# A decoder on one core: the scan layer L3_attn woven batch by batch into the steps of the slot layer L2_ffn

## The chip, the core and the metric

The kernel runs on 1 core of one Trainium2 chip. The time is the device time of one launch in microseconds. The kernel before took 3780.62 us (median of 3 runs, 3766.05 to 3781.16).

## What is computed

Four decoder levels of three layers each, one after another, on x of 8 batches x 256 tokens x 256 features in fp32. Every layer adds its result for layernorm(x) to x. The change concerns two neighbours: the slot layer L2_ffn, and the scan layer L3_attn behind it.

```python
# L2_ffn, X = layernorm(x); 1024 slots, hidden width 1024
xn, se = rms_norm(X, gamma_x), rms_norm(slot_embeds, gamma_slot)
logits = einsum('bsd,etd->bset', xn, se)
dispatch = softmax(logits, axis=1)                   # over the tokens
slots = einsum('bsd,bset->betd', xn, dispatch)
processed = gelu(slots @ w1) @ w2
combine = softmax(logits.reshape(b, s, e * t), axis=-1)   # over the slots
x = x + einsum('bnd,bsn->bsd', processed, combine)

# L3_attn, X = layernorm(x)
Z = layernorm(X) * gamma + beta
A = sigmoid(Z @ Wa.T + ba)
P = cumprod(A, axis=1)
S = cumsum((Z @ Wb.T + bb) / (P + 1e-8), axis=1)
x = x + (Z @ Wc.T + bc) * (P * (h0 + S)) + X
```

Both layers are independent from batch to batch. Within a batch, the scan needs the finished x of the slot layer.

## The kernel before

Everything stays in on-chip memory; one function for each layer and engine is written out in the engine's own queue, and every order between engines is a semaphore. `sig.up(name)` raises one, `sig.at(name, lane, trip, n)` is the value to wait for. There is no scheduler: the order in each queue is the order of the code. `Chain.link` (used for short dependent operations on VectorE) raises a semaphore and waits for it on the same engine. PSUM has 8 banks of 128 x 512 fp32 (`k.ps`).

**The slot layer** works in steps. A step finishes batch e (its inner products) and starts batch f = e + 1 (its logits and softmaxes). TensorE's pieces alternate between the two:
- `hidden_tensor`: slots @ w1, eight outputs for each half of the slots, in banks 4 and 5 by turns; ScalarE reads each with Gelu (`gelu_scalar`, L3320).
- `slot_zT_tensor` (L351): four transposes of f's normalized batch into bank 0.
- `logits_tensor`: banks 0 to 3; VectorE takes their maxima (L3400) and copies them (L3402), ScalarE takes the exponentials (L3338), VectorE scales them (L3404, L3405).
- `logits_turn_tensor` and `dispatch_turn_tensor` (L3226), 16 transposes each: logits, and dispatch weights; VectorE takes maxima (L3408), ScalarE the combine weights (L3344); both engines copy the turned dispatch weights (L3351, L3414).
- `processed_tensor`: hidden @ w2 in banks 6 and 7, four outputs a half, copied by VectorE (L3382).
- `slots_tensor`, `combine_turn_tensor` (L3264), and `combined_tensor`: the result in bank 6, which VectorE adds to x (L3421) ahead of its copy of combine weights (L3428).

A first step starts batch 0, a hardware loop (`Fori`) runs seven steps, a last one finishes batch 7. On VectorE a step opens with f's layernorm (L335) and RMS norm (L3156 to L3161, with the reciprocal root by ten short operations, L268 to L272).

**The scan layer** begins when all of x is there: statistics of the last tiles, the norms of all 16 tiles in one go (`norms_vector`), then a loop of four trips with two batches each, in banks 0 to 3 and 4 to 7. For each batch: a layernorm from those norms (L335), a second one (L279 to L288), four transposes (L351), two reads by ScalarE (L3494), 12 matmuls for a, b and c (L360), six reads by ScalarE (L3502), and on VectorE two running products (L3529), an addition, a reciprocal (L3532), a product, two running sums (L3535), L3538 and L3541; four transposes back (L3482), and two additions (L3546, L3547). The next layer, L3_xattn, starts with `norms_vector` again (L317, L324).

Nearly all matmuls go through one helper, so they have one line: `proj_feature` and `products` record L360. A matmul of fp32 operands is two records in the trace; a transpose is one.

## Time and profile before

| | |
|---|---|
| median of 3 runs | 3780.62 us |
| the profiled execution: device time, span | 3774.22 us, 3772.3 us |
| TensorE busy | 3108.0 us (82%) |
| VectorE busy | 1841.8 us (49%) |
| ScalarE busy | 1276.4 us (34%) |
| GpSimd busy | 439.8 us (12%) |
| mean granted TensorE clock | 0.897 |

Times inside the execution are microseconds from the start of its span. The slot layer's seven looped steps run from about 2537 to 3128, its last one to 3194, the scan layer from there to 3363. PE is TensorE (PEld its weight loads), DVE VectorE, ACT ScalarE, SP SyncE, which issues the DMAs. A busy share is an average over stages with different limits; the change is in one stretch, so its windows and its timeline say more. A granted clock of 1.00 is 2.4 GHz, 0.50 is 1.2 GHz, and what lies between is a mean over a stretch with both.

### The profile page before, as it was taken

The numbers are of one execution on the slowest core, as the hardware profiler recorded it, in microseconds if no ns is written. First come the engines' busy times: TensorE is split into PE (matmuls) and PEld (weight loads), VectorE is DVE, ScalarE is ACT, GpSimd is POOL, SyncE is SP. The second block draws the span as 40 slices with busy tenths as digits, with TensorE's granted clock in tenths as the row PEclk, the third lists the DMA queues.
The fourth block names the chain that finished last, engine by engine and source line by source line (L and its number), as shares of the span: only waits on it lengthen the run. The fifth ranks groups of instructions, "written<-read, shape, count | busy, mean of one in ns | idle before, by whom it ended". The sixth has DMA issues, their size and how long they took to land.

```text
span 3772.3 us, 54488 instructions
## 1 busy us (share of the span) xinstructions
PE 3108.0 (82%) x21063; PEld 2108.0 (56%) x21063; DVE 1841.8 (49%) x6353; ACT 1276.4 (34%) x2052; POOL 439.8 (12%) x454
## 2 busy tenths in 40 slices
PE   6999999589888788688862898959999998449877
PEld 3666668455554455455541565636666665336665
DVE  4443433699883466534449686542222221663323
ACT  1222213255554232133320686423233221224333
POOL 0001011123333000000001565000000000000000
PEclk9999999789898898799985899989999999669877
DMA  2000000100000000000000101000000000000000
GB/s 108 1 1 1 1 1 1 44 1 2 1 1 29 27 1 1 1 1 1 1 4 16 28 25 42 2 9 1 0 0 0 0 0 14 0 7 2 1 11 11
DMA packets 21697, 37.38 MB, mean 10 GB/s; under 512 B 2084, under 2 KB 19685, under 8 KB 20456
## 3 DMA queue, kind: packets, MB, share of 16 engines
q1 hardware_dynamic: 20664, 34.02, 2.7%
q8 instruction: 145, 2.38, 0.3%
q14 instruction: 72, 0.59, 0.1%
q10 hardware_dynamic: 816, 0.39, 0.0%
...
## 4 chain that ended last, share of the span: by engine, by line
PE 67%; DVE 22%; ACT 5%; issue 4%; DVEq 0%; SPq 0%; DMA 0%; POOL 0%; ACTq 0%; POOLq 0%
PE ps L360 38%; DVE arena L509 3%; DVE arena L1552 2%; PE ps L555 2%; ACT arena L590 2%; PE ps L457 2%; PE ps L2658 2%; PE ps L2001 2%; PE ps L2047 2%; PE ps L2677 2%; PE ps L602 2%; DVE arena L1543 2%; PE ps L643 2%; PE ps L1235 1%; PE ps L494 1%
## 5 line engine op out<-in xcount | busy, mean ns | idle before, releaser
L360 PE MATMUL ps<-weights,arena 128*128 128x256 f32 (+6 forms) x2592 | 722.2, 428 | 23.6 <-ACT arena L1369 7.6
L360 PE MATMUL ps<-arena,weights 128*128 128x256 f32 (+4 forms) x1936 | 611.9, 469 | 37.5 <-DMA fp_bias<-in_fp_bias 27.4
L360 PEld LDWEIGHTS ps<-weights,arena 128*128 128x128 f32 (+2 forms) x2592 | 484.7, 199 | 201.1 <-issue 110.3
L360 PEld LDWEIGHTS ps<-arena,weights 128*128 128x128 f32 (+1 forms) x1936 | 384.6, 209 | 225.1 <-issue 121.7
L360 PE MATMUL ps<-arena 128*128 128x256 f32 (+3 forms) x1592 | 416.0, 416 | 48.7 <-DVE arena L1822 43.4
L360 PEld LDWEIGHTS ps<-arena 128*128 128x128 f32 (+2 forms) x1592 | 297.3, 189 | 154.4 <-issue 68.1
L509 DVE TENSOR_REDUCE arena<-ps 128x16 f32<-128x1232 f32 (+2 forms) x96 | 179.1, 1866 | 204.4 <-PE ps L479 56.9
L590 ACT ACTIVATE arena<-ps 77x2048 f32<-77x2048 f32 (+1 forms) x112 | 209.9, 1874 | 171.6 <-PE ps L555 154.9
L1552 DVE MATCH_REPLACE8 arena<-arena 128x77 f32<-128x77 f32 x1024 | 215.2, 227 | 0.0
L771 POOL TENSOR_TENSOR x<-x,weights 128x512 f32<-128x512 f32 x32 | 40.7, 1272 | 1448.0 <-DVE arena L737 1448.0
L2014 ACT ACTIVATE arena<-ps 128x1536 f32<-128x1536 f32 x128 | 185.5, 1451 | 58.4 <-PE ps L2003 51.0
L643 PE MATMUL ps<-ident,arena 128*128 128x128 f32 x480 | 89.5, 316 | 106.3 <-DVE arena L737 41.8
L2032 POOL TENSOR_SCALAR_AFFINE_SELECT arena<-arena 128x512 f32<-128x512 f32 x128 | 152.5, 1192 | 116.6 <-ACT arena L2014 115.8
L1543 DVE MAX8 arena<-arena 128x8 f32<-128x77 f32 x1024 | 149.9, 227 | 11.4 <-ACT arena L1097 11.4
L351 PE MATMUL ps<-ident,arena 128*128 128x128 f32 x192 | 46.3, 398 | 118.2 <-DVE arena L288 45.9
L643 PEld LDWEIGHTS ps<-ident,arena 128*128 128x128 f32 x480 | 59.5, 158 | 147.7 <-issue 113.1
L3382 DVE COPY arena<-ps 128x1024 f32<-128x1024 f32 x16 | 19.6, 1225 | 244.7 <-PE ps L360 244.7
L555 PE MATMUL ps<-arena 32*77 32x256 f32 (+2 forms) x1792 | 131.7, 394 | 0.0
L2023 DVE TENSOR_TENSOR arena<-arena 128x512 f32<-128x512 f32 x128 | 88.4, 691 | 75.1 <-ACT arena L2014 74.3
L3320 ACT ACTIVATE arena<-ps 128x512 f32<-128x512 f32 x128 | 75.7, 597 | 130.3 <-PE ps L360 130.1
L457 PE MATMUL ps<-masks,identb 128*128 128x256 bf16 (+1 forms) x384 | 79.5, 333 | 48.6 <-DVE arena L509 26.6
L2001 PE MATMUL ps<-arena 12*128 12x256 bf16 x512 | 103.5, 279 | 10.0 <-DMA arena<-arena 9.8
...
## 6 DMA issues: line engine op xcount, KB each, us to landing
...
weights<-in_w_L_ffn SPq DMA_DIRECT2D x1, 3848.0 KB, 11.5
...
```

Of the source, the lines that this page charges most:

```text
L360: ins = k.nc.tensor.matmul(out, lhsT, rhs, start=start and i == 0, stop=i == n - 1)
L457: k.nc.tensor.matmul(out, k.identb[:, :], mask, start=True, stop=False, skip_group_check=True)
L509: k.nc.vector.tensor_reduce(out, src, AX, ALU.max).then_inc(*s.sig.up(u.a.p + "top"))
L555: ins = k.nc.tensor.matmul(k.ps[0:u.a.nk, HI + i, out], kT[group(i)], qT[group(i)], start=False, stop=True, skip_group_check=True)
L590: k.nc.scalar.activation(out, k.ps[0:u.a.nk, HI:HI + 4, :], ACT.Exp, scale=u.a.scale)\
L643: ins = k.nc.tensor.transpose(out[:, (2 * c + t) * P:(2 * c + t + 1) * P], src[:, t, c * P:(c + 1) * P], k.ident[:, :])
L1543: ins = v.max(tops_of_half(s, t, half, i)[:, h, :], of_half(s, t, half)[:, h, :])
L1552: ins = v.match_replace(left, tops_of_half(s, t, half, i)[:, h, :], left, -BIG)
L2001: mm(k.ps[:, base + u // 2, u % 2 * SEQ:(u % 2 + 1) * SEQ], kk[:, 0:P], q, start=True, stop=True, skip_group_check=True)
L2014: k.nc.scalar.activation(s.prob[at % PROBS], k.ps[:, base:base + 3, :].rearrange("p b f -> p (b f)"), ACT.Exp, scale=NH1 ** -0.5).then_inc ...
L2023: k.nc.vector.tensor_tensor(diag, diag, s.seen.unsqueeze(1).broadcast_to([P, 4, P]), ALU.min)\
L2032: k.nc.gpsimd.affine_select(diag, diag, [[0, 4], [1, P]], ALU.is_ge, 0.0, base=0, channel_multiplier=-1)\
```

## The change

The scan layer's own stage is gone, with its norms over all tiles. The slot layer is written out in ten steps instead of a loop: step `s` finishes batch e = s - 1, starts batch f = s, and carries the scan of batch n = s - 2, each where it exists. So steps 2 to 7 carry all three, step 8 carries e = 7 and n = 6, step 9 only n = 7. The scan of a batch calculates both layernorms itself. Its transposed z goes to bank 7, a and b to banks 4 and 5 (once the last gelu of the half has read them), c to bank 4 once a has been read, and the result's transposes to bank 4. `done` is now raised by the scan's last addition, the slot layer's own one raises `slotted`. The statistics of the finished batch for the next layer are taken at its end, so that L3_xattn takes none itself. SyncE loads the weights of L3_xattn after the last `slotted`; TensorE waits for the scan's weights before step 0.

```diff
-    prep = Signals(k.signals, "L2_ffn", 1, 1, se=1, seT_ps=1, seT=1, done=1, dve_step=k.steps["slots_prep"])
+    prep = Signals(k.signals, "L2_ffn", 1, 1, se=1, seT_ps=1, seT=1, dve_step=k.steps["slots_prep"])
     sig = Signals(k.signals, "L2_ffn", B, 1, z=1, zT_ps=1, zT=1, lT_ps=1, ex=1, l=1, l_ps=1, cmax=1, comb=1,
                   disp=1, dispT_ps=1, dispT_a=1, dispT_v=1, slots_ps=1, slots=1, combT_ps=1, combT_a=1, combT_v=1,
-                  hid_ps=16, hid=16, proc_ps=2, proc=2, out_ps=1, done=1, dve_step=k.steps["L2_ffn"])
-    return Bag(norms=norms, buf=buf, prep=prep, sig=sig)
+                  hid_ps=16, hid=16, proc_ps=2, proc=2, out_ps=1, slotted=1, dve_step=k.steps["L2_ffn"],
+                  g_z=1, g_zT_ps=1, g_zT=1, g_ab_ps=1, g_a=1, g_b=1, g_c_ps=1, g_c=1, g_o=1, g_out_ps=1,
+                  g_step=34, done=1, stats=1)
+    k.stats_ready["L3_attn"] = sig.at("stats", 0, B - 1, 1)
+    return Bag(norms=norms, buf=buf, g=g, prep=prep, sig=sig)
...
             pe.wait_ge(*s.sig.at("slots", 0, e, 1))
+            if e >= 2:
+                pe.wait_ge(*s.sig.at("done", 0, e - 2, 1))
+        if n == 8 and e:
+            pe.wait_ge(*s.sig.at("g_b", 0, e - 1, 1))
+            pe.wait_ge(*s.sig.at("g_c", 0, e - 1, 1))
...
-            pe.wait_ge(*s.sig.at("done", 0, e, 0))
+        elif e:
+            pe.wait_ge(*s.sig.at("slotted", 0, e - 1, 1))
...
+def scan_z_tensor(k, pe, s, n):
+    pe.wait_ge(*s.sig.at("g_z", 0, n, 1))
+    turn_tensor(k, s.g.zn, k.ps[:, 7, :]).then_inc(*s.sig.up("g_zT_ps"))
+def scan_in_tensor(k, w, src, b):
+    for c in range(KC):
+        ins = proj_feature(k, k.ps[:, b, c * SEQ:(c + 1) * SEQ], w_of(k, "L3_attn", w, KC), src, c * P, P)
+    return ins
+def scan_ab_tensor(k, pe, s, n):
+    pe.wait_ge(*s.sig.at("g_zT", 0, n, 1))
+    if n + 1 < B:
+        pe.wait_ge(*s.sig.at("hid", 0, n + 1, 8))
+    scan_in_tensor(k, "wa", s.g.zT, 4)
+    scan_in_tensor(k, "wb", s.g.zT, 5).then_inc(*s.sig.up("g_ab_ps"))
+def scan_c_tensor(k, pe, s, n):
+    pe.wait_ge(*s.sig.at("g_a", 0, n, 1))
+    scan_in_tensor(k, "wc", s.g.zT, 4).then_inc(*s.sig.up("g_c_ps"))
+def scan_out_tensor(k, pe, s, n):
+    pe.wait_ge(*s.sig.at("g_o", 0, n, 1))
+    if n + 1 < B:
+        pe.wait_ge(*s.sig.at("hid", 0, n + 1, 16))
+    for t in (0, 1):
+        for c in range(KC):
+            ins = k.nc.tensor.transpose(k.ps[:, 4, (2 * t + c) * P:(2 * t + c + 1) * P],
+                                        s.g.b[:, c, t * P:(t + 1) * P], k.ident[:, :])
+    ins.then_inc(*s.sig.up("g_out_ps"))
...
-    enter(k, pe, s.sig)
-    slots_step_tensor(k, pe, s, None, 0, first=True)
-    with pe.Fori(0, B - 1) as trip:
-        slots_step_tensor(k, pe, s, trip, trip + 1)
-    slots_step_tensor(k, pe, s, B - 1, None)
+    pe.wait_ge(*s.prep.at("seT", 0, 0, 1))
+    pe.wait_ge(*k.loaded["L3_attn"])
+    for step in range(B + 2):
+        e, f, n = in_steps(step - 1), in_steps(step), in_steps(step - 2)
+        if e is not None:
+            hidden_tensor(k, pe, s, e, 0, 0, 4)
+        if f is not None:
+            slot_zT_tensor(k, pe, s, f)
+        if e is not None:
+            hidden_tensor(k, pe, s, e, 0, 4, 8)
+        if n is not None:
+            scan_z_tensor(k, pe, s, n)
+        if f is not None:
+            logits_tensor(k, pe, s, f)
+        if n is not None:
+            scan_ab_tensor(k, pe, s, n)
+        if e is not None:
+            processed_tensor(k, pe, s, e, 0, 0, 2)
+        if n is not None:
+            scan_c_tensor(k, pe, s, n)
+        if e is not None:
+            processed_tensor(k, pe, s, e, 0, 2, 3)
+        if f is not None:
+            logits_turn_tensor(k, pe, s, f)
+        if e is not None:
+            processed_tensor(k, pe, s, e, 0, 3, 4)
+            hidden_tensor(k, pe, s, e, 1, 0, 4)
+        if f is not None:
+            dispatch_turn_tensor(k, pe, s, f)
+        if e is not None:
+            hidden_tensor(k, pe, s, e, 1, 4, 8)
+        if f is not None:
+            slots_tensor(k, pe, s, f)
+        if e is not None:
+            processed_tensor(k, pe, s, e, 1, 0, 4)
+        if n is not None:
+            scan_out_tensor(k, pe, s, n)
+        if f is not None:
+            combine_turn_tensor(k, pe, s, f)
+        if e is not None:
+            combined_tensor(k, pe, s, e)
...
+def scan_z_scalar(k, act, s, n):
+    act.wait_ge(*s.sig.at("g_zT_ps", 0, n, 1))
+    for c in range(KC):
+        ins = k.nc.scalar.activation(s.g.zT[:, c, :], k.ps[:, 7, c * SEQ:(c + 1) * SEQ], ACT.Identity,
+                                     bias=col_of(k, "L3_attn_be", c), scale=col_of(k, "L3_attn_g", c))
+    ins.then_inc(*s.sig.up("g_zT"))
+def scan_in_scalar(k, dst, b, fn, bias):
+    for c in range(KC):
+        ins = k.nc.scalar.activation(dst[:, c, :], k.ps[:, b, c * SEQ:(c + 1) * SEQ], fn, bias=col_of(k, bias, c))
+    return ins
+def scan_ab_scalar(k, act, s, n):
+    act.wait_ge(*s.sig.at("g_ab_ps", 0, n, 1))
+    if n:
+        act.wait_ge(*s.sig.at("g_out_ps", 0, n - 1, 1))
+    scan_in_scalar(k, s.g.a, 4, ACT.Sigmoid, "L3_attn_ba").then_inc(*s.sig.up("g_a"))
+    scan_in_scalar(k, s.g.b, 5, ACT.Identity, "L3_attn_bb").then_inc(*s.sig.up("g_b"))
+def scan_c_scalar(k, act, s, n):
+    act.wait_ge(*s.sig.at("g_c_ps", 0, n, 1))
+    scan_in_scalar(k, s.g.c, 4, ACT.Identity, "L3_attn_bc").then_inc(*s.sig.up("g_c"))
...
+            gelu_scalar(k, act, s, e, 0, 4, 8)
+        if n is not None:
+            scan_z_scalar(k, act, s, n)
+            scan_ab_scalar(k, act, s, n)
...
+            ins.then_inc(*sig.up("ex"))
+        if n is not None:
+            scan_c_scalar(k, act, s, n)
...
+def scan_z_vector(k, dve, s, n, ch):
+    v, g = k.nc.vector, s.g
+    tiles = [k.xs[:, SPARE + 2 * n + t, :] for t in (0, 1)]
+    dve.wait_ge(*s.sig.at("slotted", 0, n, 1))
+    if n:
+        dve.wait_ge(*s.sig.at("done", 0, n - 1, 1))
+        dve.wait_ge(*s.sig.at("g_zT_ps", 0, n - 1, 1))
+    for src, dst in ((tiles, g.z), ([g.z[:, 0, :], g.z[:, 1, :]], g.zn)):
+        hold(k, dve, "vector")
+        for t in (0, 1):
+            ins = v.bn_stats(g.st[:, t, :], src[t])
+        ch.link(ins)
+        hold(k, dve, "vector")
+        for t in (0, 1):
+            ins = v.bn_aggr(g.mv[:, t, :], g.st[:, t, :])
+        ch.link(ins)
+        ch.link(v.tensor_scalar(g.var, g.mv[:, :, 1], LN_EPS, None, ALU.add))
+        rsqrt(k, ch.link, g.rstd, g.var, g.t)
+        hold(k, dve, "vector")
+        for t in (0, 1):
+            ins = v.tensor_scalar(dst[:, t, :], src[t], g.mv[:, t, 0:1], g.rstd[:, t:t + 1], ALU.subtract, ALU.mult)
+        if dst is g.z:
+            ch.link(ins)
+    ins.then_inc(*s.sig.up("g_z"))
+def scan_sums_vector(k, dve, s, n, ch, part):
+    v, g = k.nc.vector, s.g
+    if part == 0:
+        dve.wait_ge(*s.sig.at("g_a", 0, n, 1))
+        for c in range(KC):
+            ins = v.tensor_tensor_scan(g.prod[:, c, :], g.a[:, c, :], g.ones, 1.0, ALU.mult, ALU.mult)
+        ch.link(ins)
+        ch.link(v.tensor_scalar(flat(g.a), flat(g.prod), 1e-8, None, ALU.add))
+        ch.link(v.reciprocal(flat(g.a), flat(g.a)))
+    else:
+        dve.wait_ge(*s.sig.at("g_b", 0, n, 1))
+        ch.link(v.tensor_tensor(flat(g.a), flat(g.b), flat(g.a), ALU.mult))
+        for c in range(KC):
+            ins = v.tensor_tensor_scan(g.sum[:, c, :], g.a[:, c, :], g.ones, 0.0, ALU.add, ALU.mult)
+        ch.link(ins)
+        for c in range(KC):
+            ins = v.scalar_tensor_tensor(g.b[:, c, :], g.sum[:, c, :], col_of(k, "L3_attn_h0", c), g.prod[:, c, :],
+                                         ALU.add, ALU.mult)
+        ch.link(ins)
+        dve.wait_ge(*s.sig.at("g_c", 0, n, 1))
+        v.tensor_tensor(flat(g.b), flat(g.b), flat(g.c), ALU.mult).then_inc(*s.sig.up("g_o"))
+def scan_done_vector(k, dve, s, n, ch):
+    v, g, x = k.nc.vector, s.g, x_at(k, n)
+    dve.wait_ge(*s.sig.at("g_out_ps", 0, n, 1))
+    ch.link(v.tensor_tensor(g.z, g.z, k.ps[:, 4, :].rearrange("p (t d) -> p t d", t=2), ALU.add))
+    v.tensor_tensor(x, x, g.z, ALU.add).then_inc(*s.sig.up("done"))
+    ch.close()
+    batch_stats_vector(k, dve, s, n)
...
+            rms_vector(k, ch, buf.z, buf.zn, buf.sq, buf.norm, 2).then_inc(*sig.up("z"))
+        if n is not None:
+            scan = Chain(dve, sig, 0, n, "g_step")
+            scan_z_vector(k, dve, s, n, scan)
...
+            processed_vector(k, dve, s, e, 0)
+        if n is not None:
+            scan_sums_vector(k, dve, s, n, scan, 0)
+        if f is not None:
+            dve.wait_ge(*sig.at("dispT_ps", 0, f, 1))
+            v.tensor_copy(buf.disp[:, 1, :], flat(k.ps[:, 2:4, :])).then_inc(*sig.up("dispT_v"))
+        if n is not None:
+            scan_sums_vector(k, dve, s, n, scan, 1)
+        if e is not None:
+            processed_vector(k, dve, s, e, 1)
+        if n is not None:
+            scan_done_vector(k, dve, s, n, scan)
```

Lines of the new kernel that the pieces below name: L3241 and L3279 are the old L3226 and L3264; L643 is the turn of the scan's z, L3316 the turn of its result; L3467 is the old L3382, L3572 the old L3414.

TensorE, the middle of a step. Before, in the loop, from the last matmuls of the first hidden half to the turn of the logits:

```order
L360 MATMUL ps<-arena,weights 128x512 x2
L360 MATMUL ps<-arena 128x256 x16
L3185 REGISTER_ALU
L3189 REGISTER_ALU
L360 MATMUL ps<-weights,arena 128x256 x24
L3232 REGISTER_ALU
L3226 MATMUL ps<-ident,arena 128x128 x16
L360 MATMUL ps<-weights,arena 128x256 x8
```

Now, in step 2, the same stretch:

```order
L360 MATMUL ps<-arena,weights 128x512 x8
L643 MATMUL ps<-ident,arena 128x128 x4
L360 MATMUL ps<-arena 128x256 x16
L360 MATMUL ps<-arena,weights 128x256 x8
L360 MATMUL ps<-weights,arena 128x256 x16
L360 MATMUL ps<-arena,weights 128x256 x4
L360 MATMUL ps<-weights,arena 128x256 x8
L3241 MATMUL ps<-ident,arena 128x128 x16
L360 MATMUL ps<-weights,arena 128x256 x8
```

The turn of the scan's z stands ahead of the logits, the eight matmuls of a and b behind them, and the four of c inside the inner products.

VectorE, between the maxima of the turned logits and the copies of inner products. Before:

```order
L3408 TENSOR_REDUCE arena<-ps 128x2
L3381 REGISTER_ALU
L3382 COPY arena<-ps 128x1024
L3413 REGISTER_ALU
L3414 COPY arena<-ps 128x1024
L3381 REGISTER_ALU
L3382 COPY arena<-ps 128x1024
```

Now, in step 2 (the first form of L3504 and L3512 are the running product and sum):

```order
L3564 TENSOR_REDUCE arena<-ps 128x2
L3467 COPY arena<-ps 128x1024
L3504 SCALAR_TENSOR_TENSOR arena<-arena 128x256 x2
L3506 TENSOR_SCALAR arena<-arena 128x512
L3507 RECIPROCAL arena<-arena 128x512
L3572 COPY arena<-ps 128x1024
L3510 TENSOR_TENSOR arena<-arena 128x512
L3512 SCALAR_TENSOR_TENSOR arena<-arena 128x256 x2
L3515 SCALAR_TENSOR_TENSOR arena<-arena,cols 128x256 x2
L3519 TENSOR_TENSOR arena<-arena 128x512
L3467 COPY arena<-ps 128x1024
```

The scan's sums stand in two parts, around the copy of the turned dispatch weights.

ScalarE, from the first half's gelus to the combine weights. Now, in step 2; before, L3338 with its table load stood directly behind the gelus, and L3344 behind L3338:

```order
L3378 ACTIVATE arena<-ps 128x512 x4
L3384 ACTIVATE arena<-ps,cols 128x256 x2
L3391 ACT_TABLE_LOAD
L3391 ACTIVATE arena<-ps,cols 128x256 x4
L3434 ACT_TABLE_LOAD
L3434 ACTIVATE arena<-arena 128x256 x8
L3391 ACTIVATE arena<-ps,cols 128x256 x2
L3443 ACTIVATE arena<-ps,arena 128x1024 x2
```

The reads of z, a and b stand ahead of the exponentials (now L3434), the read of c ahead of the combine weights (now L3443).

## Rows read from the trace of the kernel before

**Rows 1.** The profile's page: shares of the chain that ended last, by engine.

```profile
PE 67%; DVE 22%; ACT 5%; issue 4%; DVEq 0%; SPq 0%; DMA 0%; POOL 0%; ACTq 0%; POOLq 0%
```

**Rows 2.** Windows: stretch, length, busy time of each engine, clock, DMA share, GB/s.

```profile
2876.50:2960.70 84.20, 81.99 (x326) 56.90 (x325) 20.32 (x32) 24.66 (x46) 0.00 (x0) 1.00 0.00 0
3204.80:3245.50 40.70, 16.81 (x65) 13.48 (x66) 29.65 (x68) 9.20 (x18) 0.00 (x0) 0.67 0.00 0
3204.80:3210.50 5.70, 2.01 (x8) 1.61 (x9) 5.10 (x23) 1.02 (x2) 0.00 (x0) 0.50 0.00 0
3210.50:3217.70 7.20, 7.20 (x27) 6.07 (x26) 0.36 (x2) 2.31 (x3) 0.00 (x0) 0.74 0.00 0
2160.00:2220.00 60.00, 59.73 (x822) 37.44 (x822) 48.10 (x73) 48.39 (x40) 38.02 (x32) 1.00 0.09 24
```

**Rows 3.** Waits of one slot step, 2876.5 to 2960.7: total us, times, longest.

```profile
DVE arena L3400 <- PE ps L360: 14.0, 1, 14.0
...
DVE arena L3414 <- PE ps L3226: 8.0, 1, 8.0
DVE x L3421 <- PE ps L360: 7.7, 1, 7.7
...
PE ps L351 <- DVE arena L3161: 1.9, 1, 1.9
```

**Rows 4.** Timeline of that slot step: start, us, engine, line, work, [idle before].

```profile
2878.76 0.74 DVE L335 TENSOR_SCALAR arena<-x,norm,rstd 128x256 f32 x2 [1.02 <-issue]
...
2883.15 0.62 DVE L3161 TENSOR_SCALAR arena<-arena 128x256 f32<-128x256 f32 x2
...
2883.99 0.65 PE L351 MATMUL ps<-ident,arena 128*128 128x128 f32 x4 [1.87 <-DVE arena L3161]
...
2891.35 7.07 PE L360 MATMUL ps<-arena 128*128 128x256 f32 x32
...
2898.26 10.52 PE L360 MATMUL ps<-weights,arena 128*128 128x256 f32 x48
...
2902.98 0.51 ACT L3338 ACTIVATE arena<-arena 128x256 f32<-128x256 f32 x1 [9.53 <-DVE arena L3402]
...
2908.62 1.91 PE L3226 MATMUL ps<-ident,arena 128*128 128x128 f32 x16
...
2915.81 1.28 ACT L3320 ACT_TABLE_LOAD   x1 [0.62 <-PE ps L360]
...
2917.10 1.09 ACT L3320 ACTIVATE arena<-ps 128x512 f32<-128x512 f32 x2
...
2917.76 3.70 PE L360 MATMUL ps<-arena,weights 128*128 128x512 f32 x8 [0.34 <-ACT arena L3320]
```

**Rows 5.** Timeline of the last slot step's end and the scan stage.

```profile
3142.22 14.08 PE L360 MATMUL ps<-weights,arena 128*128 128x256 f32 x64 [0.69 <-ACT arena L3320]
...
3193.48 0.88 DVE L3421 SCALAR_TENSOR_TENSOR x<-ps,arena,x 128x256 f32<-128x256 f32 x2 [7.41 <-PE ps L360]
...
3200.68 0.75 DVE L279 BATCH_NORM_STATS2 arena<-arena 128x6 f32<-128x256 f32 x2
...
3204.04 0.73 DVE L288 TENSOR_SCALAR arena<-arena 128x256 f32<-128x256 f32 x2
...
3204.83 1.11 PE L351 MATMUL ps<-ident,arena 128*128 128x128 f32 x4 [11.50 <-DVE arena L288]
...
3205.98 1.02 ACT L3494 ACTIVATE arena<-ps,cols 128x256 f32<-128x256 f32 x2 [5.24 <-PE ps L351]
...
3220.04 1.28 DVE L3529 TENSOR_TENSOR_SCAN arena<-arena 128x256 f32<-128x256 f32 x2 [9.18 <-ACT arena L3502]
...
3228.90 1.12 PE L3482 MATMUL ps<-ident,arena 128*128 128x128 f32 x4 [6.03 <-DVE arena L3541]
...
3361.94 0.69 DVE L3547 TENSOR_TENSOR x<-x,arena 128x512 f32 x1
...
3365.19 1.17 DVE L324 BATCH_NORM_AGGREGATE norm<-stats 128x2 f32<-128x6 f32 x16 [0.15 <-DVE stats L317]
```

More of the change, by code:

```diff
@@ L3365, in L2_ffn_scalar @@
-def L2_ffn_scalar(k, act, s):
-    a = k.nc.scalar.activation
     enter(k, act, s.prep)
@@ L3436, in L2_ffn_vector @@
     enter(k, dve, s.prep)
     norms_vector(k, dve, s.norms)
[L3438 removed]
+    v.memset(buf.m, 0.0)
+    v.memset(s.g.ones, 1.0)
+    rms_vector(k, prep, buf.slots, buf.slots, buf.out, buf.norm, SC).then_inc(*s.prep.up("se"))
     dve.wait_ge(*s.prep.at("seT", 0, 0, 1))
[L3440 to L3443 removed]
@@ L3444, in L2_ffn_vector @@
-    with dve.Fori(0, B - 1) as trip:
-        slots_step_vector(k, dve, s, trip, trip + 1)
-    slots_step_vector(k, dve, s, B - 1, None)
-def scan_plan(k):
-    c, bufs = lane_buffers(k)
-    for buf in bufs:
-        buf.zn = c.take(2, D)
-        buf.a, buf.b, buf.c = c.take(KC, SEQ), c.take(KC, SEQ), c.take(KC, SEQ)
-        buf.prod, buf.sum = c.take(KC, SEQ), c.take(KC, SEQ)
-    ones = c.take(SEQ)
-    norms = norms_plan(k, "L3_attn")
-    prep = Signals(k.signals, "L3_attn", 1, 1, done=1)
-    sig = Signals(k.signals, "L3_attn", B // 2, 2, z=1, zT_ps=1, zT=1, abc_ps=1, abc=1, o=1, out_ps=1, done=1,
-                  dve_step=k.steps["L3_attn"])
-    return Bag(norms=norms, bufs=bufs, ones=ones, prep=prep, sig=sig)
```

302 lines of the change are left out of this document (90 added, 212 removed).

## Prediction

> **What bounds the kernel now.** I read the chain that ended last first: it runs through TensorE for 67% of the span and through VectorE for 22% [rows 1]. So a change counts where it shortens TensorE's own stream, or a place where TensorE waits for VectorE. Next the windows of the two stages that are woven together. In a slot step of 84.2 us TensorE is busy for 82.0 us at a granted clock of 1.00, VectorE for 20.3 and ScalarE for 24.7; in a trip of the scan stage, 40.7 us for two batches, TensorE is busy for 16.8 us at 0.67 and VectorE, with 29.7 us, leads [rows 2]. The first stage is a full TensorE beside an idle VectorE, the second a chain between engines. Then the waits of a slot step: VectorE waits 14.0, 8.0 and 7.7 us for TensorE at its reads of logits (L3400), turned dispatch weights (L3414) and output (L3421); TensorE waits once for VectorE, 1.9 us, for z [rows 3]. The timeline last, for where each new piece falls.
>
> **What goes.** From VectorE's add at the end of the last slot step (3193.48) to the norms of the next layer (L324 at 3365.19) it is 171.7 us [rows 5]. After the change the same stretch holds one batch's scan alone (step 9). The rest of the scan work has to fit into eight slot steps.
>
> **Step 9, one scan alone.** From the last slot add: 0.9 for the add and 0.15 for the hold behind it. Two layernorms: one runs from 3200.68 to the end of L288 at 3204.77, 4.1 us [rows 5], so 8.2; each new pass has a hold ahead of its statistics and one ahead of its apply, which I estimate at 0.12 each from the 0.15 that stands idle ahead of L324 [rows 5], so 8.7. Transposes 1.1 and ScalarE's copy 1.0 [rows 5]. The products for a and b are 16 matmul records. TensorE has been idle about 10 us by then, as it was for 11.5 us before the row at 3204.83, after which the granted clock was 0.50 for 5.7 us and 0.74 over the next 7.2, that is about 3.7 us at 1.2 GHz and the rest at 2.4 [rows 2, 5]. A record takes 0.216 us at full clock (48 between 2898.26 and 2908.62 [rows 4]), 0.43 at half: 3.7 us give 8.6 records, the other 7.4 take 1.6, together 5.3 (bounds 3.5 and 6.9). Sigmoid 0.9; the two reads of the same size at 3205.98 take 1.02. VectorE's sums from scan to product, 3220.04 to the transposes at 3228.90, 8.9 [rows 5]. Transposes 1.1, two adds 1.4 (L3547 takes 0.69), then the rest up to L324: today 2.6 from the end of the last add (3362.63) to 3365.19 with four statistics in it, of which two are left, so 1.7: 1.05 + 8.7 + 1.1 + 1.1 + 5.3 + 0.9 + 8.9 + 1.1 + 1.4 + 1.7 = 31.3 us; with links, 31.5 (29.5 to 34). The product with c hides behind the sums. Gain here: 171.7 - 31.5 = 140.2 us.
>
> **A full step (steps 2 to 7, six of them).** TensorE gets 24 records of 0.216, 5.2 us, and eight transposes of 0.11 (16 between 2908.62 and the next matmul take at most 1.9 [rows 4]), 0.9: 6.1 us. TensorE is busy for 97% of a step, so all of it lengthens the step; banks 4, 5 and 7 are free at those places. Waits:
> - z of the slot batch. VectorE idles 1.0 us at the top of a loop trip (L335 at 2878.76) and TensorE then 1.87 us for it at 2883.99 [rows 4]. Without a loop I leave about 0.2 of the 1.0: 0.8 us gained.
> - z of the scan batch is new. Its 8.7 us stand right behind the slot batch's z, which ended at 2883.77 and will at 2883.0; so it is there at 2891.7, and 0.2 later TensorE can start. TensorE arrives there 0.8 before 2891.35, at 2890.6: a wait of 1.3 us (bounds 0 and 2.6). Behind this wait stand the logits, which need nothing of it.
> - ScalarE. Products for a and b end 3.4 us behind the logits; sigmoid and identity take 1.8, the switch to Exp 1.3, so Exp starts at logits + 6.6, where it was + 4.7 (2902.98 against 2898.26 [rows 4]). Exponentials, maxima and combine weights move back by 2 us, but TensorE's turn of the logits moves back by 5.2 (a, b and c stand ahead of it), so that it still sets the maxima. Combine weights end at logits + 22.1, the first hidden product at + 22.4: today ScalarE reads it after a table load that waits for it (2915.81, [rows 4]); in the new order that load waits only for the inner products and starts at 22.1. TensorE's 0.34 us wait at 2917.76 and the pause of its weight loads there shrink: 0.3 gained.
> - VectorE's sums. The first half (scan, add, reciprocal: about 5.2 of the 8.9 us) stands behind the copy of the inner products, in the 8.0 us that VectorE waits ahead of L3414; the second half (3.7) behind that copy, where nothing is late; the two adds and the statistics (2.4) in the 7.7 us ahead of L3421 [rows 3]. Nothing on the path; without that cover each would cost its length.
> Sum: 6.1 - 0.8 + 1.3 - 0.3 = 6.3, and 0.2 less for the rests of the loop that TensorE's and ScalarE's queues had: 6.1 us a step (4.8 to 8), 36.6 for six.
>
> **Step 8** has no slot batch ahead of the scan's z, so that comes in time. TensorE waits instead for ScalarE's 0.8 us copy with its semaphores, 1.3 us, has 3.4 + 1.7 for its products and 0.4 for the transposes ahead of them; the transposes behind fall into the wait for VectorE's last copy. The new products cover the 0.69 us for the last gelu (3142.22, [rows 5]). 6.2 us (5 to 7.5).
>
> **Steps 0 and 1** carry no scan: -1.0 us (a z that comes earlier, and a memset and waits gone). The load of the scan's weights and SyncE's queue stand as they did.
>
> **The sum.** -140.2 + 36.6 + 6.2 - 1.0 = -98.4 us. On the profiled execution's own 3774.2 us that is 3675.8. The median of the three runs is 6.4 above the profiled execution, their lowest 8.2 below, so I put the median between, at 3679.
>
> **A page that speaks against it.** ScalarE changes tables three times in a step, before and after (the load at the loop's top goes, one ahead of the sigmoid comes), but two of the three then stand where ScalarE has little time to spare. In this trace the load at 2915.81 takes 1.28 us and the activation starts at 2917.10, 0.01 us behind its end [rows 4]. The Trainium skill (ScalarE: Activation LUTs, What ACT_TABLE_LOAD costs) gives the same 1283 ns, but adds about 1380 ns of drain to every switch. By that page, the switch to Exp and the next to Gelu would each be later by 1.4 us, TensorE would wait some 2.8 us more in a step, and the sum would end near 3696; the trace doesn't bear the drain out.
>
> **Rivals.**
> - ScalarE becomes late. Its queue has a and b ahead of Exp and c ahead of the combine weights. The margin is thin: combine weights at 22.1, first hidden product at 22.4. If ScalarE's new pieces take 2 us more (a load of 1.28 that is not hidden ahead of the sigmoid, and 0.7 of semaphores), TensorE waits 2 us a step at its third hidden product: 6 x 2 = 12, 3691. For it: the four waits between engines in a row. Against: 9.5 us idle ahead of Exp today [rows 4].
> - TensorE's clock. If the new pause made it fall, each step would lose what the spell at 0.50 to 0.74 cost: 3.7 us at half clock lose 1.9 us of work [rows 2]. Once or twice a step that is 11 to 22 us: 3690 to 3701. Against: with a pause of 1.87 us in each step the clock stands at 1.00.
> - No new wait. VectorE is ready before TensorE, and a step costs 4.8: 3671.
> - Slower than before: VectorE's queue in series. The scan's layernorms stand ahead of the logits' maxima and its sums ahead of the copies that TensorE's dispatch needs. The place from which it decides: 171.7 - 31.5 - 6.2 + 1.0 = 135 us over six steps, 22.5 us a step. All of VectorE's new work is 8.7 + 8.9 + 2.4 = 20.0; were all of it on the path beside TensorE's 6.1, a step would grow by 26.1 and the kernel end at 3799. Against: 29.7 us of idle at three places of the same step [rows 3].
> - The unrolled code is not there in time for an engine. At 5 us a step, 3714. Against: a stage with 822 matmul records in 60 us, written out too, keeps TensorE busy for 59.7 [rows 2].
>
> **How the numbers follow.** Forecast 0.64 (own range 3661 to 3695: six steps at 4.8 to 8, step 9 at 29.5 to 34, step 8 at 5 to 7.5, and the runs' own spread of 8 us each way, not all at once); ScalarE late 0.13; clock 0.07; no new wait 0.08; code late 0.04; VectorE in series 0.03; 0.01 that nothing moves. The range of 3656 to 3702 leaves out the last three and the ends of the others. Half a percent, 19 us, is what a measurement can tell from no change: all cases but the last two lie below 3762. Faster 0.95, same 0.02, slower 0.03.
>
> **What would show it.** Slot steps 2 to 7 of about 90.3 us with TensorE busy for 88; a wait of 1.3 us ahead of the turn of the scan's z; no wait of TensorE for ScalarE over 0.5 us in a step; VectorE busy for about 40 us a step and still idle ahead of the logits; clock 1.00 in all of them; about 31.5 us from the last slot add to the norms of the next layer, with the products for a and b in some 5.3 us. The prediction is wrong if steps take over 92.5 us or under 88.5, if the clock leaves 1.00 in them, or if the tail is over 36.

## The result, and the profile after

The changed kernel takes 3674.5 us (median of 4 runs, 3660.4 to 3678.5) against 3780.9 us (4 runs, 3766.1 to 3784.4): the ratio is 0.972 (95% interval 0.968 to 0.976). The forecast was 3679, with a range of 3656 to 3702. The profiled execution took 3674.57 us with a span of 3672.6, where the one of before took 3774.22 with 3772.3, so 99.7 us are to be explained (the medians are 106.4 apart).

The first view is again the chain that ended last, by engine. It looks as it did [rows 1], because it covers 3.7 ms and the change touches a quarter of that:

```profile
PE 67%; DVE 23%; ACT 5%; issue 3%; SPq 0%; DMA 0%; POOL 0%; DVEq 0%; ACTq 0%; POOLq 0%
```

The second is the windows (length, busy time of PE, PEld, DVE, ACT and POOL, clock, DMA share, GB/s): a full step, step 8, and step 9 up to the norms of the next layer.

```profile
2805.15:2894.90 89.75, 88.01 (x357) 62.19 (x356) 37.04 (x77) 28.20 (x54) 0.00 (x0) 1.00 0.00 1
3164.20:3235.80 71.60, 68.72 (x256) 47.37 (x254) 22.19 (x54) 16.41 (x27) 0.00 (x0) 1.00 0.00 0
3235.80:3266.90 31.10, 9.61 (x32) 7.02 (x32) 19.03 (x57) 4.71 (x9) 0.00 (x0) 0.75 0.15 46
```

Against the slot step of before [rows 2] a full step has 31 matmul records and 6.0 us of TensorE more, and is 5.6 us longer. VectorE does 16.7 us more in it and ScalarE 3.5. Of both only one piece shows in the length: the wait of 0.93 us for the scan's z, further down. The clock is at 1.00, as before.

The third is the waits of that step (total us, times, longest). VectorE's three waits for TensorE are there still [rows 3], the one ahead of L3572, formerly L3414, down from 8.0 to 2.4, since the sums now stand there. TensorE has two waits of under 1 us, both for a z.

```profile
DVE arena L3556 <- PE ps L360: 7.7, 1, 7.7
...
DVE x L3584 <- PE ps L360: 5.8, 1, 5.8
...
DVE arena L3572 <- PE ps L3241: 2.4, 1, 2.4
...
PE ps L643 <- DVE arena L3492: 0.9, 1, 0.9
...
PE ps L351 <- DVE arena L3171: 0.8, 1, 0.8
```

The fourth is the timeline of the same step (start, us, engine, line, work, [idle before]), where the rows answer to those of [rows 4].

```profile
2812.01 0.62 DVE L3171 TENSOR_SCALAR arena<-arena 128x256 f32<-128x256 f32 x2
...
2812.69 0.66 PE L351 MATMUL ps<-ident,arena 128*128 128x128 f32 x4 [0.81 <-DVE arena L3171]
...
2820.36 0.74 DVE L3492 TENSOR_SCALAR arena<-arena 128x256 f32<-128x256 f32 x2 [0.15 <-DVE arena L272]
...
2821.15 0.66 PE L643 MATMUL ps<-ident,arena 128*128 128x128 f32 x4 [0.93 <-DVE arena L3492]
2821.64 7.07 PE L360 MATMUL ps<-arena 128*128 128x256 f32 x32
...
2833.81 1.28 ACT L3434 ACT_TABLE_LOAD   x1
2835.10 0.51 ACT L3434 ACTIVATE arena<-arena 128x256 f32<-128x256 f32 x1
...
2850.70 1.28 ACT L3378 ACT_TABLE_LOAD   x1
2851.99 0.60 ACT L3378 ACTIVATE arena<-ps 128x512 f32<-128x512 f32 x1
...
2858.20 1.23 DVE L3572 COPY arena<-ps 128x1024 f32<-128x1024 f32 x1 [2.44 <-PE ps L3241]
```

The slots' z ends at 2812.63 and the scan's at 2821.10, 8.5 us later. TensorE stands at the turn of the scan's z (L643) for the last 0.93 us of that. Nowhere does it wait for ScalarE.

The last is the timeline from the last slot update on, which answers to [rows 5]:

```profile
3235.81 0.88 DVE L3584 SCALAR_TENSOR_TENSOR x<-ps,arena,x 128x256 f32<-128x256 f32 x2 [5.18 <-PE ps L360]
...
3245.48 1.11 PE L643 MATMUL ps<-ident,arena 128*128 128x128 f32 x4 [9.83 <-DVE arena L3492]
3246.64 1.02 ACT L3384 ACTIVATE arena<-ps,cols 128x256 f32<-128x256 f32 x2 [33.63 <-PE ps L643]
...
3247.71 5.38 PE L360 MATMUL ps<-arena,weights 128*128 128x256 f32 x16 [1.11 <-ACT arena L3384]
...
3254.00 1.27 DVE L3504 TENSOR_TENSOR_SCAN arena<-arena 128x256 f32<-128x256 f32 x2 [8.57 <-ACT arena L3391]
...
3262.85 1.12 PE L3316 MATMUL ps<-ident,arena 128*128 128x128 f32 x4 [6.83 <-DVE arena L3519]
...
3266.92 1.17 DVE L324 BATCH_NORM_AGGREGATE norm<-stats 128x2 f32<-128x6 f32 x16
```

From 3235.81 to 3266.92 it is 31.1 us, where it was 171.7.

**Where the 99.7 us came from.** The whole layer is measured between the norms ahead of it and those behind it (both L324): 894.1 us before, 790.2 after. Inside it I take VectorE's slot updates as marks.

| part | before, us | after, us | change | forecast |
|---|---|---|---|---|
| norms to the first slot update | 150.1 | 148.9 | -1.2 | -1.0 |
| the six steps with everything in them | 506.9 | 538.5 | +31.6 | +36.6 |
| step 8 | 65.4 | 71.6 | +6.2 | +6.2 |
| last slot update to the next norms | 171.7 | 31.1 | -140.6 | -140.2 |
| the layer | 894.1 | 790.2 | -103.9 | -98.4 |
| all that lies ahead of it | 2471.1 | 2476.8 | +5.6 | 0 |
| all that lies behind it | 407.1 | 405.7 | -1.4 | 0 |

The layer gained 5.5 us more than forecast. The code ahead of it is the same in both kernels, and in the later profiles below it ends anywhere from 2459.9 to 2494.6, so the 5.6 us there belong to the execution and not to the change. One of the six steps of before was slow, 85.96 us where the others took 84.18 to 84.20. In it the clock fell behind the wait for z:

```profile
2629.73 0.65 PE L351 MATMUL ps<-ident,arena 128*128 128x128 f32 x4 [1.96 <-DVE arena L3161]
2630.22 8.73 PE L360 MATMUL ps<-arena,weights 128*128 128x512 f32 x16
```

The 16 matmul records of the second row take 7.03 us where the clock is at 1.00. So one step costs 89.75 - 84.18 = 5.6 us, against 6.1 forecast, and the slow step of before gives 1.8 us more.

### The profile page after: what moved, and what is told of

It is laid out like the page before. It is cut to its first block, busy times and chain, and to the rows that moved or that the text cites. A ratio compares the mean times of both kernels' runs of the same rounds, so it can differ in the third digit from the quotient of the medians.

```text
span 3672.6 us, 53702 instructions
## 1 busy us (share of the span) xinstructions
PE 3089.6 (84%) x21063; PEld 2096.1 (57%) x21063; DVE 1854.6 (50%) x6424; ACT 1273.1 (35%) x2047; POOL 440.9 (12%) x454
## 4 chain that ended last, share of the span: by engine, by line
PE 67%; DVE 23%; ACT 5%; issue 3%; SPq 0%; DMA 0%; POOL 0%; DVEq 0%; ACTq 0%; POOLq 0%
PE ps L360 38%; DVE arena L509 3%; DVE arena L1552 3%; PE ps L555 2%; DVE arena L1543 2%; ACT arena L590 2%; PE ps L457 2%; PE ps L2001 2%; PE ps L2047 2%; PE ps L2658 2%; PE ps L2677 2%; PE ps L602 2%; PE ps L643 2%; PE ps L1235 1%; PE ps L494 1%
## 5 line engine op out<-in xcount | busy, mean ns | idle before, releaser
L643 PE MATMUL ps<-ident,arena 128*128 128x128 f32 x512 | 97.4, 321 | 124.4 <-DVE arena L737 40.6
L643 PEld LDWEIGHTS ps<-ident,arena 128*128 128x128 f32 x512 | 64.8, 160 | 171.6 <-issue 115.1
L2023 DVE TENSOR_TENSOR arena<-arena 128x512 f32<-128x512 f32 x128 | 88.0, 687 | 87.8 <-ACT arena L2014 87.0
L3467 DVE COPY arena<-ps 128x1024 f32<-128x1024 f32 x16 | 19.6, 1226 | 212.7 <-PE ps L360 212.7
L3378 ACT ACTIVATE arena<-ps 128x512 f32<-128x512 f32 x128 | 76.6, 598 | 119.5 <-PE ps L360 119.4
L602 PE MATMUL ps<-arena 77*17 77x256 f32 (+2 forms) x1536 | 107.7, 388 | 0.9 <-ACT arena L590 0.9
```

Source lines behind the costliest of these rows:

```text
L602: ins = k.nc.tensor.matmul(k.ps[PAD * i:PAD * i + u.a.vw, LO + c, at:at + SEQ], v[0:nk, 0, 4 * j + i, :], s.prob[0:nk, i, j * SEQ:(j + 1) ...
L643: ins = k.nc.tensor.transpose(out[:, (2 * c + t) * P:(2 * c + t + 1) * P], src[:, t, c * P:(c + 1) * P], k.ident[:, :])
```

## The experiments

Each is the kernel after with one edit, unless it says otherwise. "Step" is the time between two slot updates in the six full steps, "tail" the time from the last one to the next norms. In the kernel after they are 89.75 and 31.1 us.

**1. Unrolling without weaving.** The change did two things: it wrote the slot loop out, and wove the scan into it. This is the kernel before with its loop alone written out, on all three engines:

```diff
-    with pe.Fori(0, B - 1) as trip:
+    for trip in range(B - 1):
...
-    with act.Fori(0, B - 1) as trip:
+    for trip in range(B - 1):
...
-    with dve.Fori(0, B - 1) as trip:
+    for trip in range(B - 1):
```

> The kernel before with the slot layer's loop written out and nothing woven; the scan keeps its own stage. My account: writing out only shortens VectorE's start of a step, so that TensorE's wait for the slot batch's z falls from 1.87 to about 0.8 us in each of the seven steps with two batches: 83.1 us a step instead of 84.2, 6 to 8 us in all, about 3767 profiled. The weaving itself then holds the other 97 us. Rival: the long code of the changed kernel is itself a good part of the gain (over 20 us), or costs something that the weaving had to pay (this kernel slower than before). A second point: one of the seven steps before lost 1.7 us at a lowered clock behind its wait of 1.96 us; with waits of 0.8 us I expect all seven alike.

Measured: 3767.4 us (10 runs), ratio 0.997 (0.994 to 1.000), which can't be told from no change. The profile tells more: a step takes 82.53 us in all six, against 84.18, and the tail 171.7 as before. VectorE's and TensorE's timeline at the top of a step, and ScalarE's around the gelu:

```profile
2796.77 0.73 DVE L335 TENSOR_SCALAR arena<-x,norm,rstd 128x256 f32<-128x256 f32 x2 [0.18 <-DVE arena L3429]
...
2801.82 0.66 PE L351 MATMUL ps<-ident,arena 128*128 128x128 f32 x4 [0.81 <-DVE arena L3161]
...
2832.83 0.20 ACT L3344 ACTIVATION_READ_ACCUMULATOR arena<-ps,arena 128x1 f32 x1
2833.04 1.28 ACT L3320 ACT_TABLE_LOAD   x1
2834.34 0.60 ACT L3320 ACTIVATE arena<-ps 128x512 f32<-128x512 f32 x1
```

Two waits go. The wait for z falls from 1.87 to 0.81, since VectorE's idle time at the top of a trip falls from 1.02 us to 0.18. And the table load for the gelu starts 0.01 us behind the combine weights, where it stood 0.6 us idle and waited for a hidden product [rows 4]; TensorE's 0.34 us wait for that gelu is gone, and TensorE's busy time falls by 0.3 (82.0 to 81.7). A table load that no wait of TensorE shows goes too, one of 1.28 us at the top of each trip (2876.33 in the kernel before). Unrolling is worth 1.65 us a step, about 12 of the layer's 104 us (894.1 to 882.4, the slow step of before included). The weaving has the other 92: 882.4 to 790.2. Against this kernel a full step grows by 7.2 us: TensorE's work by 6.3 (81.7 to 88.0 busy), and 0.9 is the new wait for the scan's z.

**2. A third layernorm pass.** How much does VectorE's part in front of the turn weigh? The scan's first pass is taken twice:

```diff
-    for src, dst in ((tiles, g.z), ([g.z[:, 0, :], g.z[:, 1, :]], g.zn)):
+    for src, dst in ((tiles, g.z), (tiles, g.z), ([g.z[:, 0, :], g.z[:, 1, :]], g.zn)):
...
```

> The changed kernel with the scan's first layernorm calculated twice on VectorE (the same values again), 4.35 us more ahead of the turn of the scan's z. Account that VectorE's queue ends last there by 0.93 us: the wait of TensorE grows from 0.9 to 5.3 us in each of the six full steps, 94.1 us a step; step 8, where z is now 2.4 us early, grows by 2.0, step 9 by 4.35: 32 us in all, about 3707. If the longer pause costs TensorE its clock, another 1.7 us a step behind it, up to 3717. Rival: VectorE has cover there and only step 9 grows: 3679.

Measured: 3729.6 us (4 runs), ratio 0.985 (0.981 to 0.989); a step 95.5 to 95.8, step 8 76.6, the tail 36.5. TensorE's timeline, and a window around it:

```profile
2858.08 1.11 PE L643 MATMUL ps<-ident,arena 128*128 128x128 f32 x4 [5.28 <-DVE arena L3492]
2858.99 8.20 PE L360 MATMUL ps<-arena 128*128 128x256 f32 x32
```

```profile
2853.00:2862.00 9.00, 3.92 (x13) 3.40 (x14) 4.20 (x19) 2.74 (x4) 0.00 (x0) 0.81 0.00 1
```

The wait grows by 4.35 us, a whole pass: in a full step nothing hides any more of VectorE's work ahead of that turn. The rest is the clock. Behind a pause of 5.3 us it falls, the turn takes 0.45 and the logits 1.13 us longer, together 1.6 us in every step: 4.35 + 1.6 = 5.95. So the prediction's clock rival had something to it: the pause of 0.93 us that two passes leave costs itself alone, the one that three leave costs 1.6 us on top of itself.

Step 8 grew by 5.0 us, where I had expected 2.0, and that is the clock again:

```profile
3235.69 0.66 PE L643 MATMUL ps<-ident,arena 128*128 128x128 f32 x4 [1.86 <-DVE arena L3492]
```

Behind this pause, the turn, and 1.11 us for ScalarE's copy the clock stood at 0.50 from 3237.4 to 3242.4, and the a/b products took 6.5 us. In the tail, z comes 4.35 us later and the a/b products take 6.42 us where they took 5.38: 5.4 together. So the layer grew by 48.7 us (790.2 to 838.9), and the time lies above the 3717 that I had put as the most.

**3. The scan's turn behind the logits.** The logits need nothing of the scan, so that TensorE can do them first:

```diff
-        if n is not None:
-            scan_z_tensor(k, pe, s, n)
         if f is not None:
             logits_tensor(k, pe, s, f)
+        if n is not None:
+            scan_z_tensor(k, pe, s, n)
+        if e is not None:
+            processed_tensor(k, pe, s, e, 0, 0, 1)
         if n is not None:
             scan_ab_tensor(k, pe, s, n)
         if e is not None:
-            processed_tensor(k, pe, s, e, 0, 0, 2)
+            processed_tensor(k, pe, s, e, 0, 1, 2)
```

> The changed kernel with TensorE's turn of the scan's z behind the logits instead of ahead of them, and the products for a and b behind the first output of the inner products. Account: z of the scan is then 6 us early, the copy by ScalarE has an inner product as cover, and the wait of 0.93 us goes in six steps, and about 0.8 net in step 8: 88.8 us a step, 6 us less, about 3668. ScalarE's exponentials start 3.9 us later and the maxima still wait for TensorE's turn. Rival: ScalarE's chain (a and b, then exponentials, then VectorE's scaling) becomes late for the turn or the maxima, and steps stay at 89.8 or grow: 3675 or more.

Measured: 3660.1 us (4 runs), ratio 0.970 (0.966 to 0.974); a step 88.6, step 8 70.7, the tail 31.6.

```profile
2795.96 0.66 PE L351 MATMUL ps<-ident,arena 128*128 128x128 f32 x4 [0.81 <-DVE arena L3171]
2796.46 7.03 PE L360 MATMUL ps<-arena,weights 128*128 128x512 f32 x16
2803.33 7.07 PE L360 MATMUL ps<-arena 128*128 128x256 f32 x32
2810.24 0.60 PE L643 MATMUL ps<-ident,arena 128*128 128x128 f32 x4
```

The wait ahead of L643 is gone, and the step is shorter by 1.15 us: the 0.93 of the wait, and 0.2 of TensorE's busy time (88.0 to 87.8), of which the trace shows 0.06 in the turn (0.66 to 0.60). Step 8 gains 0.9: its wait of 1.16 us for ScalarE's copy is gone, and one of 0.25 for a gelu is new. Together 8 us in the layer, of which the runs' medians can't be sure.

**4. More work for ScalarE.** Two exponentials of 128x1024 into a tile that nothing reads, in front of the combine weights:

```diff
...
+            for t in (0, 1) if n is not None else ():
+                a(s.g.more[:, t, :], flat(k.ps[:, 2 * t:2 * t + 2, :]), ACT.Exp, bias=buf.m[:, 2 * SC + t:2 * SC + t + 1])
```

> The changed kernel with two more exponentials of 128x1024 on ScalarE in each step that carries a scan, ahead of the combine weights (results unused), 2.1 us more. Account that ScalarE has a margin of about 0.2 us at the first gelu of the second half: TensorE waits about 1.9 us more in each of the six full steps, 91.6 us a step, 11 us in all, about 3686. Rival: ScalarE has real room there: steps stay at 89.8 and the time at 3675.

Measured in one run: 3683.0 us; a step 91.76, step 8 unchanged (it has no combine weights), the tail 31.9.

```profile
2855.00 3.70 PE L360 MATMUL ps<-arena,weights 128*128 128x512 f32 x8 [1.75 <-ACT arena L3378]
```

Of 2 x 1.12 = 2.24 us added, 2.0 show in the step. ScalarE's margin in a full step is thus some 0.2 us. That it is close to the prediction's 0.3 (22.1 and 22.4 behind the logits) is partly luck: ScalarE can read the first hidden product only behind the load, 1.28 us after 22.1. What counts is how much earlier the load starts. By [rows 4] it started as the first hidden product came, 17.55 us behind the logits (2915.81 against 2898.26), which 5.2 us of new work make 22.75, and TensorE then waited 0.34 us for the gelu. From 22.1 the load starts 0.6 earlier; that takes away the 0.34 and leaves 0.3. The rival of a late ScalarE failed by that margin only.

**5. More work for VectorE, further down.** The reciprocal of 3.35 us is taken twice:

```diff
...
+        ch.link(v.reciprocal(flat(g.sum), flat(g.a)))
         ch.link(v.reciprocal(flat(g.a), flat(g.a)))
```

> The kernel after, with the scan's reciprocal (3.4 us on VectorE) taken twice in every step, the first time into scratch. VectorE is 37 us busy in a step of 89.75. Theory of the prediction: VectorE's part of the scan lies beside TensorE in a full step, so 3.4 us more there is taken up by the idle time ahead of the slot update (2.4 us ahead of its first addition) and by what TensorE still has to do: steps stay at 89.8, at most 90.8; step 8 stays at 71.6; only step 9, where nothing runs beside it, grows, 31.1 to 34.5. Time 3678. Rival, the slower case of the prediction in small: VectorE's work in a step is in series with TensorE's, so every step grows by 3.4, the time by 8 x 3.4 = 27 to 31: 3702 or more.

Measured in one run: 3675.8 us; a step 89.75, step 8 71.6, the tail 34.7. VectorE in a full step:

```profile
2938.08 3.35 DVE L3507 RECIPROCAL arena<-arena 128x512 f32<-128x512 f32 x1
2941.47 3.35 DVE L3508 RECIPROCAL arena<-arena 128x512 f32<-128x512 f32 x1
2944.85 1.23 DVE L3573 COPY arena<-ps 128x1024 f32<-128x1024 f32 x1
```

The copy (L3573 here) no longer waits and comes about 1 us later in the step; TensorE does not ask for it yet, and the step stays as it was to the hundredth. Experiments 2 and 5 both add to VectorE's work in the same step: 4.35 us cost 5.9 ahead of the turn, and 3.35 cost nothing behind it. In the tail, where nothing runs beside them, both cost their length or more, 5.4 and 3.6.

**6. TensorE kept at work in step 9.** Matmuls of the identity whose results nothing reads, 10 ahead of the turn of the last scan's z and 8 ahead of the turn of its result:

```diff
+def warm_tensor(k, s, times):
+    for i in range(times):
+        k.nc.tensor.matmul(k.ps[:, i % 4, :], k.ident[:, :], s.buf.slotsT[:, 0, 0:512], start=True, stop=True)
...
+        if n == B - 1:
+            warm_tensor(k, s, 10)
         if n is not None:
             scan_z_tensor(k, pe, s, n)
...
+        if n == B - 1:
+            warm_tensor(k, s, 8)
         if n is not None:
             scan_out_tensor(k, pe, s, n)
```

> The kernel after, with 18 more 128x128 by 512 matmuls of the identity whose results nothing reads, in step 9 alone: 10 ahead of the turn of the scan's z and 8 ahead of the turn of its result, while TensorE waits there (9.8 us and about 15 us). Theory: after the last slot update TensorE's three groups run slow because it has stood idle ahead of them; with work directly ahead the z turn takes about 0.5 us instead of 1.11, the a/b products 3.6 instead of 5.4, the result's turn 0.6 instead of 1.13, and the stretch from the last slot update to the norms of the next layer falls from 31.1 to 28 to 29 us; steps stay at 89.75. Rival: the chain there is VectorE's and ScalarE's, and the group's length is that of 16 weight loads, so that nothing moves: 31.1. Second rival: the clock does not come back within 10 products: 31 to 32. Time 3671 or 3674.

Measured in one run: 3662.8 us, 11.8 under the profiled execution of the kernel after. The layer has only 0.9 of it; 4.9 lie ahead of it and 5.9 behind, in code that is the same. The tail took 30.2 us, not the 28 to 29 expected.

```profile
3240.54 0.66 PE L643 MATMUL ps<-ident,arena 128*128 128x128 f32 x4 [1.24 <-DVE arena L3501]
...
3242.30 5.41 PE L360 MATMUL ps<-arena,weights 128*128 128x256 f32 x16 [1.11 <-ACT arena L3393]
...
3257.49 0.66 PE L3321 MATMUL ps<-ident,arena 128*128 128x128 f32 x4
```

```profile
3240.50:3241.20 0.70, 0.66 (x4) 0.42 (x4) 0.00 (x0) 0.00 (x0) 0.00 (x0) 1.00 0.00 0
3241.20:3242.30 1.10, 0.00 (x0) 0.00 (x0) 0.00 (x0) 1.05 (x3) 0.00 (x0) 1.00 0.00 0
3242.30:3243.30 1.00, 1.00 (x3) 0.84 (x4) 0.00 (x0) 1.00 (x1) 0.00 (x0) 0.72 0.00 0
3243.30:3244.30 1.00, 1.00 (x4) 0.78 (x3) 0.00 (x0) 0.25 (x1) 0.00 (x0) 0.50 0.00 0
```

Both turns came down from 1.11 to 0.66 as expected. The a/b products (16 records) did not: 5.41 against the 3.6 expected. The clock held through the turn and fell then, to 0.50, which is 1.2 GHz, behind two pauses of 1.24 and 1.11 us with the short turn between them. Experiment 9 filled those as well.

**7. The slots' turn one group later.** On top of the third experiment, the hidden products ahead of the turn of the slots' z are split 5 and 3, and the gelu passes with them:

```diff
-            hidden_tensor(k, pe, s, e, 0, 0, 4)
+            hidden_tensor(k, pe, s, e, 0, 0, 5)
...
-            hidden_tensor(k, pe, s, e, 0, 4, 8)
+            hidden_tensor(k, pe, s, e, 0, 5, 8)
...
-            gelu_scalar(k, act, s, e, 0, 0, 4)
+            gelu_scalar(k, act, s, e, 0, 0, 5)
...
-            gelu_scalar(k, act, s, e, 0, 4, 8)
+            gelu_scalar(k, act, s, e, 0, 5, 8)
```

> The kernel with the scan's turn behind the logits, and the hidden products ahead of the turn of the slots' z split 5 and 3 rather than 4 and 4, so that this turn stands one group (1.7 us) later; the gelu passes follow in the same split. Theory: the only time in which TensorE waits in a full step of that kernel is 0.81 us for the second layernorm of the slots; one more group ahead of it covers that, so that a step falls from 88.6 to 87.8 and step 8 by as much: 3655 (3652 to 3659), 5 to 7 us under the kernel with the turn behind the logits. Rival: the gelu of five instead of four groups comes later and the product behind it waits for ScalarE: the 0.8 us come back as a wait on ScalarE's pass, steps 88.6 to 89.5, 3660 to 3667.

Measured: 3658.4 us (4 runs), ratio 0.968 (0.965 to 0.971); a step 87.57.

```profile
2884.80:2972.40 87.60, 87.60 (x357) 62.35 (x356) 37.09 (x78) 28.01 (x54) 0.00 (x0) 1.00 0.00 1
```

TensorE is busy from one end of the window to the other. The step is 1.03 us shorter, a little more than the wait. The layer took 776.3 us against 782.3 in the third experiment; the medians (3660.1 and 3658.4, from two sets of runs) don't tell the two apart.

**8. Both.** The kernel of 7 with the 18 products of 6:

> All of the edits that should pay together: the scan's turn behind the logits, the split of 5 and 3, and the 18 products in step 9 that keep TensorE at work. Theory: the terms add, since one is in the full steps and the other behind the last: full steps 87.8, tail 28.5: 3652 (3647 to 3657), a ratio to the kernel before of 0.966. Rival: the products in step 9 bring nothing, then as the kernel without them, 3655; or ScalarE is late in the full steps, then 3658 to 3664.

Measured: 3658.3 us (5 runs, 3646.1 to 3666.3), ratio 0.967 (0.964 to 0.969). The steps and the tail are those of its parts, 87.57 and 30.2, but the 1.1 us of the tail (31.3 in 7) don't show in the median beside the kernel of 7. The time lies just above the 3657 that I had put as the most; the tail of 28.5 in it counted on 3.6 us for the a/b products, as experiment 6 did.

**9. No pause around the turn.** Two more products ahead of the turn, and two behind it, while ScalarE copies, in the kernel of 8:

```diff
         if n == B - 1:
-            warm_tensor(k, s, 10)
+            warm_tensor(k, s, 12)
         if n is not None:
             scan_z_tensor(k, pe, s, n)
+        if n == B - 1:
+            warm_tensor(k, s, 2)
```

> The kernel of the split and the 18 idle products, with 2 more of them ahead of the turn of the scan's z in step 9 and 2 behind it, while ScalarE copies the turned z. With the 18 alone the clock had held through the turn, but fell for about 3.5 us behind two pauses of 1.24 and 1.11 us with a turn of 0.66 us between them, and the 16 a/b products took 5.4 us as before. Theory: it is the emptiness around that turn that costs the clock; with it filled the a/b products take 3.6 to 3.7 us and the stretch from the last slot update to the norms of the next layer 28.2 to 28.8 instead of 30.2. Rival: the length of these products is set by something else in the tail, ScalarE's table load beside them for one, which starts with them: 5.4 and 30.2 again. The time moves by 2 us at most, 3644 to 3658, too little to tell from the kernel without them.

```profile
3222.54 0.60 PE L643 MATMUL ps<-ident,arena 128*128 128x128 f32 x4
3222.97 1.88 PE L3286 MATMUL ps<-arena,ident 128*128 128x512 f32 x4
3224.69 3.62 PE L360 MATMUL ps<-arena,weights 128*128 128x256 f32 x16
```

The a/b products take 3.62 us, with the clock at 1.00 and ScalarE's table load beside them as before, so that it was the clock and not the load that made them 5.4. The tail took 29.1 us, not the 28.2 to 28.8 of the theory: the 12 products ahead end 0.3 us after z is there, and the two behind the turn (two records each) end later than ScalarE's copy; together they put the a/b products 0.7 us back.

The time is 3643.9 us (6 runs, 3639.9 to 3655.1), ratio 0.964 (0.961 to 0.967), the fastest kernel here. From its profile the layer took 773.5 us, 17 less than after the change, of which 13.1 are the six steps, 0.9 step 8 and 2.0 the tail (0.6 is in the steps 0 and 1). The intervals of the two ratios to the kernel before, 0.961 to 0.967 and 0.968 to 0.976, don't touch. But the layer gives only those 17 us of the 30.6 between the two medians: in the profiles 8.6 lie ahead of it and 4.6 behind, in code that is the same. And the 14.4 us to the median of the kernel of 8 are not the edit's; its tail is 1.1 shorter.

## Why the prediction was right

**What bounds it.** That a slot step is a full TensorE beside idle engines, and the scan a chain beside an idle TensorE, is what the table bears out: 140.6 us go in one place, and 37.8 come back in seven steps. Of 16.7 us of VectorE's new work a step 0.93 show in the length; the same kind of work costs its whole length in the tail (experiments 2 and 5).

**Step 9** was worked out at 31.5 and took 31.1. Its most uncertain term, the a/b products half at the low clock, was 5.3 by the estimate and 5.38 in the trace; experiment 9 showed that the clock makes it. That the two agree to 0.1 us is luck: in experiments 3, 4, 5 and 7, where the same work stands ahead of them, these products took 5.84, 6.17, 5.21 and 5.58, and the tails of 3, 4 and 7 were 31.6, 31.9 and 31.3. What was right is that about half of them run at the low clock: it stood at 0.50 for 3.4 us of them, where I had put 3.7. The two passes took 8.5 where 8.7 was put.

**A full step** was 6.1 forecast and is 5.6. By terms:
- TensorE's work: 6.1 forecast, 6.0 measured.
- The wait for the slots' z: a gain of 0.8 forecast, 1.06 measured (1.87 to 0.81). Experiment 1 shows that it comes from unrolling alone.
- The wait for the scan's z: 1.3 forecast, 0.93 measured. This is the term that was off most. I put z 8.7 us behind the slots' z and 0.2 for the link, and it was there after 8.5 with a link of 0.05. TensorE came 7.6 us behind the slots' z, as put.
- The gelu: 0.3 forecast, 0.34 measured, but the reason was wrong. I held the new order of the engines for the cause, and experiment 1, which keeps the order of before, has the load directly behind the combine weights as well. In the loop the load stood behind the wait for the product; written out, it doesn't.
- 0.2 for the rests of the loop on TensorE's and ScalarE's queues: nothing is left for it (6.02 - 1.06 + 0.93 - 0.34 = 5.55).

Of the 5.5 us that the layer gained beyond the forecast, 3.2 are thus six steps at 0.53 less, and 1.8 the slow step in the profile of before. The forecast took its step length from a typical step, but the stretch that it compared with holds a slow one.

**Step 8**: 6.2 forecast, 6.2 measured. TensorE is busy for 6.2 us more (62.5 to 68.7), and the waits change place: one of two waits of 0.69 us for a gelu is covered, the wait for VectorE's last copy falls from 1.32 to 0.88, and 1.16 us for ScalarE's copy of z is new.

**VectorE's load** was put at about 40 us a step and is 37. The 20.0 us of new work were lengths from start to end, with the holds between instructions in them; the busy time leaves those out.

**The rivals.** ScalarE late: not so, by 0.2 us (experiment 4). Clock: it stood at 1.00 in every full step, and experiment 2 shows the cost that it would have had, 1.6 us a step behind a pause of 5.3. No new wait: not so, but it can be had by another order (experiment 3). VectorE in series: refuted by experiment 5 where its sums stand, for 3.35 us more, but true of what stands ahead of the turn (experiment 2), where each microsecond more costs at least one. Code late: TensorE's waits are all accounted for by the two z.

**The page.** The switch to Exp starts at 2833.81, takes 1.28 us, and the first exponential follows 0.01 us behind it; the switch to Gelu reads the same. The drain of about 1380 ns to every switch (the Trainium skill, ScalarE: Activation LUTs, What ACT_TABLE_LOAD costs) doesn't show here. At the switch to Gelu, with a margin of 0.2 us, it would have: experiment 4 shows that what ScalarE has to do more there comes out in the step. My 2.8 us a step by that page were too many, though. The switch to Exp has room: ScalarE stands idle for 1.72 and 6.68 us behind the exponentials, and VectorE for 4.35 ahead of the maxima (L3564), so by these rows 1.4 us there would not have reached TensorE (no run tried it).
